# Sends that wait for a later product: pacing GpSimd's scatters in a fused attention and mixture-of-experts block

## The chip, the cores and the metric

The kernel runs on one core of a Trainium2 chip. The metric is the device time of one execution in microseconds, the median of three timed runs. The profile is of another execution, taken by the hardware profiler.

## The reference

Input x is 2 x 1024 tokens of 256 numbers, float32. A small vector gives six modulation rows (shift, scale and gate for each half).

```python
h = _layernorm(x) * (1 + ca) + sa
x = x + ga * attn(h)            # layernorm, causal attention with one head of 256, o_proj, residual
h = _layernorm(x) * (1 + cb) + sb
x = x + gb * ffn(h)

# ffn, on T = 2048 tokens, E = 16 experts, 4 of them for each token, H = 128
probs = softmax(xt @ w_router); top_w, top_i = top_k(probs, 4); top_w /= sum(top_w)
g = silu(xt @ we1[e]) * (xt @ we3[e]) * cw[:, e]
moe_out = sum over e of g @ we2[e]
shared = silu(xt @ ws1) * (xt @ ws3) @ ws2       # width 512
out = shared / 5 + moe_out * 4 / 5
```

## The kernel before, in words

The five engines run programs written out by hand, which meet only at semaphores. Each engine works strictly in the order of its program.

Attention runs over 16 tiles of 128 tokens. Behind each tile the router picks four experts for every token. After each group of four tiles a rank product on TensorE (`rank`, which counts `s_rank_mm` up) gives every token its place among the rows of its expert, and VectorE turns it into four row numbers (`slot_u`, semaphore `s_slots`).

GpSimd then *sends* the tokens: `send` (line 776) issues one indirect DMA for tile t and choice k. It writes 128 rows of `hrow` to the places in the DRAM table `xg_rows` that `slot_u` names. There are 16 x 4 = 64 of them, numbered n = 4t + k. The table `SENDS` puts the first 32 between steps of attention; sends 32 to 63 are issued one behind the other after it. Sends 32 to 47 are the third group (tiles 8 to 11), 48 to 63 the fourth.

Meanwhile TensorE computes the shared part in 16 units n, a block of 512 tokens and a quarter of the width each: `gate_up(n)` (12 matmuls with 512 columns, counts `s_ab`), SiLU on ScalarE, product on VectorE, `down(n)` (8 matmuls, counts `s_y`). Units 2 to 11 stand between attention and the next stage, and in this order: gate_up(3), gate_up(4), the rank product of the last group, down(2), gate_up(5), down(3), gate_up(6), and so on.

Then the routed part. The rows in `xg_rows` are sorted by expert and cut into 79 tiles of 128, two tiles a *pair*, 40 pairs. SyncE loads a pair's rows (line 645). In round n TensorE does the gate/up product of pair n (`rows_gate_up`, 12 matmuls, counts `s_rgu`), the transposes of pair n + 2's rows (`rows_back`, line 2191), the transposes of pair n - 1's product (`g_back`, line 2217) and the down product of pair n - 2 (`rows_down`). A float32 product is split in three (lines 1816 to 1818), the parts high x high, high x low and low x high. For a pair, ScalarE applies SiLU (line 1083) and copies the result y to a buffer in SBUF (line 1092, counts `s_ry`). There are four such buffers, used in a ring, and four more for the last pairs. VectorE computes `r_g` (line 1771).

GpSimd waits for `s_ry` and scatters the pair's y, one indirect DMA a tile (line 817), to the DRAM table `y_rows`, one row for each token and choice. When they have landed, `s_back` goes up and the buffer is free. SyncE loads `y_rows` back in 16 pieces, choice by choice, as soon as enough of the pairs have landed (line 672), and VectorE adds them (line 1497), three of these adds inside the last rounds of pairs; for the last block of 512 tokens TensorE adds two of the choices (line 2004) into the last shared units. VectorE scales and adds to x, and SyncE writes the result.

Of the kernel before, what the change touches and what calls it, by code (L numbers as in the profile page):

```python
# [82 lines left out]
NPAIR = NTL // 2  # L83
# [9 lines left out]
def tiles_of(n):  # L93

    return range(1 if n == NPAIR - 1 else 2)


def loads_of(n):


    return sum(len(tiles_of(m)) for m in range(n % RING, n + 1, RING))


def products(n):


    return sum(1 + len(tiles_of(m)) for m in range(n + 1))

OWN = 6
# [22 lines left out]
NG = TILES // BT  # L134
# [59 lines left out]
SENDS = {9: 4, 10: 4, 11: 4, 12: 4, 13: 4, 14: 4, 15: 4, 16: 4}  # L194
# [41 lines left out]
def adaln_block(nc, x, qkv, o_proj, gamma, beta, w_router, we1, we3, we2, ws1, ws3, ws2, c_in, wmod, out):  # L236
# [3 lines left out]
    with ctx:  # L240
        def sem(name):
            return ctx.enter_context(nc.semaphore(name))
# [253 lines left out]
        def done(eng, stage_, t):  # L496

            if t >= 0:
                eng.wait_ge(tl[stage_], t + 1)
# [4 lines left out]
        s_chosen, s_carry, s_rank_mm, s_slots, s_tv, s_places_mm, s_places = (sem(n) for n in (  # L504
            "chosen", "carry", "rank_mm", "slots", "tile_values", "places_mm", "places"))
# [5 lines left out]
        s_ab, s_y, s_silu, s_g, s_gated, s_shared = (sem(n) for n in (  # L511
            "gate_up_mm", "down_mm", "silu", "g", "shared_gated", "shared_added"))
# [5 lines left out]
        s_rxT, s_rxhi, s_rxlo, s_rgu, s_rsilu, s_rg, s_rgT, s_rghi, s_rglo, s_rdown, s_ry = (sem("r_" + n) for n in (  # L518
            "xT", "xhi", "xlo", "gate_up", "silu", "g", "gT", "ghi", "glo", "down", "y"))
# [29 lines left out]
        def y_of(n):  # L549

            if n < NPAIR - RING:
                return y_sb[:, n % RING]
            return y_own[:, n - (NPAIR - RING)]
# [134 lines left out]
        def _(pool):  # L688
# [73 lines left out]
                                        ).then_inc(tl["resid"], 1)  # L762

            sent = [0]

            def send(count):


                for n in range(sent[0], sent[0] + count):
                    t, k = divmod(n, TOPK)  # L770
                    if n == 0:
                        pool.wait_ge(s_regions, 16 * 5)
                    if k == 0:
                        done(pool, "h2row", t)
                        pool.wait_ge(s_slots, t // BT + 1)
                    nc.gpsimd.indirect_dma_start(  # L776
                        out=xg, out_offset=bass.IndirectOffsetOnAxis(ap=slot_u[:, t, k:k + 1].bitcast(U32), axis=0),
                        in_=hrow[:, t, :], in_offset=None).then_inc(s_sent, 16)
                sent[0] += count

            for s in range(FIRST, LAST + 2):
                if -3 < s < 0:
                    residual(s + 3)
                for m, group in enumerate(norms_of(s)):
                    if s == -3 and m == 1:
                        residual(0)
                    inverse_std(group)
                    for n, t in reversed(group):
                        if n > 1:
                            mean_shift(n, t)  # L790
                if 0 <= s and s + 3 < RESIDUAL_BY_VECTOR:

                    done(pool, "rinv", s - 1)
                    residual(s + 3)
                if s == 3:
                    router_constants()
                if s == 5:
                    token_numbers()
                send(SENDS.get(s, 0))
# [5 lines left out]
            for r in range(RING):  # L805
                nc.gpsimd.memset(sent_all[:, :, r:r + 1], 16.0 * loads_of(NPAIR - RING + r)).then_inc(s_mark_const, 1)
            send(TILES * TOPK - sent[0])


            for n in range(NPAIR):  # L810
                r = n % RING

                pool.wait_ge(s_ry, n + 1)
                if n >= NPAIR - RING:
                    pool.wait_ge(s_back[r], 16 * loads_of(n - RING))
                for i in tiles_of(n):
                    nc.gpsimd.indirect_dma_start(  # L817
                        out=yb, out_offset=bass.IndirectOffsetOnAxis(ap=dest[:, 2 * n + i:2 * n + i + 1].bitcast(U32), axis=0),
                        in_=y_of(n)[:, i, :], in_offset=None).then_inc(s_back[r], 16)
# [1474 lines left out]
```

## Time and profile before

| | |
|---|---|
| timed runs, median of 3 | 339.18 us (338.8 to 339.65) |
| profiled execution, first to last instruction | 380.7 us |
| profiled execution, any other time of it | none on the page |
| TensorE busy | 333.3 us, 88% |
| VectorE busy | 255.2 us, 67% |
| ScalarE busy | 190.3 us, 50% |
| GpSimd busy | 200.8 us, 53% |
| sends of tokens (line 776) | 64, 1.02 us each |
| sends of y (line 817) | 79, 0.98 us each |

The profiled execution is 41.5 us longer than the median of the timed runs. Busy time counts an instruction from start to end, and ends of matmuls are modelled. A wait is put down to the engine that by the profile came last; "remote" is a wait whose releaser the profile does not show.

### The profile page before, as it was taken

What the parts mean: (1) busy time and instruction counts of PE and PEld (TensorE: products, weight loads), DVE (VectorE), ACT (ScalarE), POOL (GpSimd) and SP (SyncE); (2) the same over time, 40 slices, a digit from 0 to 9 for tenths busy, and PEclk for the clock granted to TensorE, in tenths of its full rate; (3) what the DMA queues carried; (4) which work ended last, traced back from release to release, by engine and by line L of the source; (5) the groups of instructions that cost most, each with busy time, mean ns of one, the idle gap of its engine ahead of it and who ended that gap; (6) DMA issues with size and microseconds to landing.
All of it is one profiled execution on the core that took longest, in us unless ns stands there. A gap on an engine that the chain in (4) does not pass through costs nothing.

```text
span 380.7 us, 7758 instructions
## 1 busy us (share of the span) xinstructions
PE 333.3 (88%) x2252; PEld 297.6 (78%) x2252; DVE 255.2 (67%) x806; ACT 190.3 (50%) x440; POOL 200.8 (53%) x285
## 2 busy tenths in 40 slices
PE   8989999999999999868889897788778877887995
PEld 5778898888899898736778796777667767877784
DVE  1889998999887756219986744543454345448797
ACT  2667777767865665414234444443444355346300
POOL 2687754357867655746740064555455545545820
PEclk9999999999999999969999999999999999999999
DMA  8236600002213996322232466556445544788824
GB/s 271 75 104 205 209 17 27 16 31 87 85 65 118 316 312 214 119 85 78 104 117 76 121 209 183 155 171 194 149 124 171 164 133 136 264 302 327 261 86 165
DMA packets 42280, 57.55 MB, mean 151 GB/s; under 512 B 5144, under 2 KB 34592, under 8 KB 42240
## 3 DMA queue, kind: packets, MB, share of 16 engines
q1 hardware_dynamic: 34288, 35.42, 30.7%
q0 software_dynamic: 6864, 19.80, 13.5%
q10 hardware_dynamic: 1088, 1.84, 1.5%
q8 instruction: 20, 0.33, 0.4%
q14 instruction: 20, 0.16, 0.2%
HBM read 32.64 MB, written 24.40 MB: 150 GB/s over the span
## 4 chain that ended last, share of the span: by engine, by line
PE 43%; DVE 27%; issue 13%; another core or an unknown queue 7%; ACT 7%; DMA 1%; POOL 1%; DVEq 0%; ACTq 0%
PE ps L1816 10%; PE ps L1818 10%; PE ps L1817 9%; PE ps L1990 4%; DVE y_in L1497 3%; DVE r_g L1771 2%; DVE gT_lo L1759 2%; ACT r_silu L1083 2%; DVE negmax L1626 2%; PE ps L2191 2%; PE ps L2092 1%; PE ps L1823 1%; DMA wmod_sb<-in_L_wmod_dram 1%; DVE bn L1197 1%
## 5 line engine op out<-in xcount | busy, mean ns | idle before, releaser
L817 POOL DMA_INDIRECT y_rows<-y_sb,aside x72 | 70.5, 980 | 87.9 <-ACT y_sb L1092 71.7
L776 POOL DMA_INDIRECT xg_rows<-hrow,slot_u x64 | 65.6, 1024 | 27.8 <-issue 20.0
L1816 PE MATMUL ps<-rpool 128*128 128x256 f32 (+3 forms) x152 | 49.8, 328 | 2.7 <-DVE rpool L1221 1.1
L1768 DVE TENSOR_TENSOR aside<-ends,aside 128x2 int32<-128x2 int32 (+1 forms) x40 | 6.3, 157 | 62.9 <-ACT r_silu L1083 55.4
L1816 PE MATMUL ps<-w_hi_routed,xT_hi 128*128 x158 | 45.2, 286 | 1.8 <-DVE xT_lo L1752 1.8
L1083 ACT ACTIVATE r_silu<-ps 128x256 f32<-128x256 f32 x40 | 15.8, 395 | 61.4 <-PE ps L1818 51.4
L1818 PE MATMUL ps<-rpool 128*128 128x256 f32 (+3 forms) x152 | 46.0, 302 | 0.0
L1817 PE MATMUL ps<-rpool 128*128 128x256 f32 (+3 forms) x152 | 45.9, 302 | 0.0
L1818 PE MATMUL ps<-w_hi_routed,xT_lo 128*128 x158 | 44.7, 283 | 0.0
L1817 PE MATMUL ps<-w_lo_routed,xT_hi 128*128 x158 | 44.6, 283 | 0.0
L1816 PE MATMUL ps<-w_hi_routed,gT_hi 128*128 x79 | 25.8, 326 | 15.1 <-DVE gT_lo L1759 15.0
L1816 PEld LDWEIGHTS ps<-rpool 128*128 128x128 f32 x152 | 28.8, 190 | 6.0 <-DVE rpool L1221 2.5
L1816 PEld LDWEIGHTS ps<-w_hi_routed,xT_hi 128*128 128x128 f32 x158 | 30.2, 191 | 2.5 <-issue 2.3
L1752 DVE TENSOR_TENSOR xT_lo<-ps,xT_hi 128x512 fp32r<-128x512 f32 x40 | 27.4, 684 | 6.2 <-ACT xT_hi L1071 6.0
L1817 PEld LDWEIGHTS ps<-w_lo_routed,xT_hi 128*128 128x128 f32 x158 | 30.2, 191 | 0.0
L1818 PEld LDWEIGHTS ps<-w_hi_routed,xT_lo 128*128 128x128 f32 x158 | 30.2, 191 | 0.0
L1816 PEld LDWEIGHTS ps<-w_hi_routed,gT_hi 128*128 128x128 f32 x79 | 14.9, 188 | 19.5 <-issue 19.4
L1818 PEld LDWEIGHTS ps<-rpool 128*128 128x128 f32 x152 | 28.8, 189 | 1.1
L1817 PEld LDWEIGHTS ps<-rpool 128*128 128x128 f32 x152 | 28.9, 190 | 0.9
L1816 PE MATMUL ps<-h2T_hi,w_hi_shared 128*128 128x512 f32 x64 | 27.3, 426 | 1.4 <-issue 0.9
L1071 ACT ACTIVATE xT_hi<-ps 128x512 fp32r<-128x512 f32 x40 | 24.4, 612 | 8.0 <-remote 5.8
L1817 PE MATMUL ps<-h2T_lo,w_hi_shared 128*128 128x512 f32 x64 | 25.6, 400 | 2.6 <-issue 2.6
(236 smaller groups left out, 928.8 us busy)
## 6 DMA issues: line engine op xcount, KB each, us to landing
xs<-xg_rows SPq DMA_DIRECT2D x68, 144.0 KB
y_in<-y_rows SPq DMA_DIRECT2D x16, 512.0 KB
xg_rows<-empty SPq DMA_DIRECT2D x4, 576.0 KB, 3.8
x_in<-in_L_attn_x_dram SPq DMA_DIRECT2D x16, 128.0 KB, 2.1
w_raw_routed<-in_L_ffn_we_dram SPq DMA_DIRECT2D x8, 256.0 KB
out_dram<-x SPq DMA_DIRECT2D x14, 128.0 KB, 1.8
xs_own<-xg_rows SPq DMA_DIRECT2D x11, 144.0 KB
wmod_sb<-in_L_wmod_dram ACTq DMA_DIRECT2D x3, 512.0 KB, 6.6
```

Source lines behind the costliest of these rows:

```text
L776: nc.gpsimd.indirect_dma_start(out=xg, out_offset=bass.IndirectOffsetOnAxis(ap=slot_u[:, t, k:k + 1].bitcast(U32), axis=0), in_=hrow[:, t, ...
L817: nc.gpsimd.indirect_dma_start(out=yb, out_offset=bass.IndirectOffsetOnAxis(ap=dest[:, 2 * n + i:2 * n + i + 1].bitcast(U32), axis=0), in_ ...
L1071: nc.scalar.activation(xT_hi[:, n % 2].rearrange("p i c t -> p (i c t)"), ps[:, 6 + n % 2, :], ACT.Copy).then_inc(s_rxhi, 1)
L1083: nc.scalar.activation(r_silu[:, n % 2], ps[:, n % 2, :].rearrange("p (i w) -> p i w", i=2)[:, :, 0:H], ACT.Silu).then_inc(s_rsilu, 1)
L1497: then(nc.vector.tensor_tensor(y[0], y[0], y[k], ALU.add))
L1626: nc.vector.tensor_reduce(negmax[:, t % 4:t % 4 + 1], score_banks(t), AX.X, ALU.max, negate=True).then_inc(tl["negmax"], 1)
L1752: nc.vector.tensor_tensor(xT_lo[:, n % 2].rearrange("p i c t -> p (i c t)"), ps[:, 6 + n % 2, :], xT_hi[:, n % 2].rearrange("p i c t -> p ...
L1759: nc.vector.tensor_tensor(gT_lo[:, n % 2].rearrange("p i t -> p (i t)"), ps[:, 2 + n % 2, 0:2 * P], gT_hi[:, n % 2].rearrange("p i t -> p ...
L1816: nc.tensor.matmul(dst, w[0], x_[0], start=first, stop=False)
L1817: nc.tensor.matmul(dst, w[0], x_[1], start=False, stop=False)
L1818: return nc.tensor.matmul(dst, w[1], x_[0], start=False, stop=last)
L1990: last = nc.tensor.matmul(to, unit(n)[1][:, tok], w_raw_s[:, e, W2:WX], start=(e == 0 and b < NB - 1 and j % 2 == 0), stop=(e == SH - 1), ...
```

## The change

Two places, both in GpSimd's program. Before the indirect DMA of sends 36, 38, 40, 42, 44 and 46 a wait is put for a product of TensorE: gate_up(2), gate_up(3), the last rank product, down(2), gate_up(5) and down(3), in this order. And the sends of pair n wait, beside `s_ry`, for the gate/up product of pair n + 3 (`s_rgu` at n + 4, for the last pairs at 40).

```diff
+PACE = 4
...
+            LATE = sum(SENDS.values())
+
+            def after_product(n):
+
+                if n == LATE + 4:
+                    pool.wait_ge(s_ab, 3)
+                if n == LATE + 6:
+                    pool.wait_ge(s_ab, 4)
+                if n == LATE + 8:
+                    pool.wait_ge(s_rank_mm, NG)
+                if n == LATE + 10:
+                    pool.wait_ge(s_y, 3)
+                if n == LATE + 12:
+                    pool.wait_ge(s_ab, 6)
+                if n == LATE + 14:
+                    pool.wait_ge(s_y, 4)
...
                         pool.wait_ge(s_slots, t // BT + 1)
+                    after_product(n)
                     nc.gpsimd.indirect_dma_start(
...
                 pool.wait_ge(s_ry, n + 1)
+                pool.wait_ge(s_rgu, min(n + PACE, NPAIR))
```

`LATE` is 32, the number of sends that the table places. No engine's order of instructions changes. What changes are the waits on GpSimd. Its program in the third and the start of the fourth group of sends, before:

```order
L802 IOTA first_of 128x40 [waits t_scores]
L806 MEMSET sent_all 128x1 x4
L776 DMA xg_rows<-hrow,slot_u 32896x288 [waits slots,t_h2row]
L776 DMA xg_rows<-hrow,slot_u 32896x288 x3
L776 DMA xg_rows<-hrow,slot_u 32896x288 [waits slots,t_h2row]
L776 DMA xg_rows<-hrow,slot_u 32896x288 x3
```

And after (`gate_up_mm`, `down_mm` and `rank_mm` are `s_ab`, `s_y` and `s_rank_mm`):

```order
L822 IOTA first_of 128x40 [waits t_scores]
L826 MEMSET sent_all 128x1 x4
L796 DMA xg_rows<-hrow,slot_u 32896x288 [waits slots,t_h2row]
L796 DMA xg_rows<-hrow,slot_u 32896x288 x3
L796 DMA xg_rows<-hrow,slot_u 32896x288 [waits gate_up_mm,slots,t_h2row]
L796 DMA xg_rows<-hrow,slot_u 32896x288
L796 DMA xg_rows<-hrow,slot_u 32896x288 [waits gate_up_mm]
L796 DMA xg_rows<-hrow,slot_u 32896x288
L796 DMA xg_rows<-hrow,slot_u 32896x288 [waits rank_mm,slots,t_h2row]
L796 DMA xg_rows<-hrow,slot_u 32896x288
L796 DMA xg_rows<-hrow,slot_u 32896x288 [waits down_mm]
```

Every second send of the third group from the fifth on is now held for a product. The sends of the first two pairs' y on GpSimd, before:

```order
L776 DMA xg_rows<-hrow,slot_u 32896x288 [waits slots,t_h2row]
L776 DMA xg_rows<-hrow,slot_u 32896x288 x3
L817 DMA y_rows<-y_sb,aside 11264x256 [waits r_y]
L817 DMA y_rows<-y_sb,aside 11264x256
L817 DMA y_rows<-y_sb,aside 11264x256 [waits r_y]
```

And after (`r_gate_up` is `s_rgu`):

```order
L796 DMA xg_rows<-hrow,slot_u 32896x288 [waits slots,t_h2row]
L796 DMA xg_rows<-hrow,slot_u 32896x288 x3
L838 DMA y_rows<-y_sb,aside 11264x256 [waits r_gate_up,r_y]
L838 DMA y_rows<-y_sb,aside 11264x256
L838 DMA y_rows<-y_sb,aside 11264x256 [waits r_gate_up,r_y]
```

The first of a pair's two sends carries the second wait; the other follows it as before.

## Rows read from the trace of the kernel before

**Rows 1.** The page, span of the profiled execution.

```profile
span 380.7 us, 7758 instructions
```

**Rows 2.** Busy time: length, PE, PEld, DVE, ACT, POOL, clock, DMA, GB/s.

```profile
0.00:158.00 158.00, 149.70 (x1032) 135.07 (x1032) 124.07 (x419) 103.49 (x251) 97.37 (x183) 1.00 0.40 134
158.00:172.00 14.00, 9.27 (x30) 6.15 (x30) 2.50 (x12) 3.65 (x6) 7.25 (x8) 0.76 0.24 91
172.00:225.00 53.00, 47.85 (x274) 41.24 (x273) 43.85 (x112) 21.96 (x39) 21.13 (x20) 1.00 0.34 109
225.00:347.00 122.00, 98.26 (x780) 91.40 (x780) 56.98 (x225) 52.92 (x128) 62.59 (x66) 1.00 0.59 189
```

**Rows 3.** Groups by line in 225:347 us: busy, mean ns | idle before, releasers.

```profile
L1092 ACT ACTIVATE y_sb<-ps 128x512 f32<-128x512 f32 x32 | 19.4, 606 | 9.3 <-PE ps L1818 8.0 <-issue 1.2
L1083 ACT ACTIVATE r_silu<-ps 128x256 f32<-128x256 f32 x32 | 12.7, 398 | 52.9 <-PE ps L1818 43.0 <-remote 9.9
```

**Rows 4.** Timeline of TensorE in the loop: start, length, instruction.

```profile
217.43 0.38 PE L2217 MATMUL ps<-ident,r_g 128*128 128x128 f32 x2
...
225.30 0.28 PE L1818 MATMUL ps<-w_hi_routed,xT_lo 128*128 x1
...
225.85 0.38 PE L2217 MATMUL ps<-ident,r_g 128*128 128x128 f32 x2
```

**Rows 5.** Timeline of ScalarE, the same stretch.

```profile
228.92 0.38 ACT L1083 ACTIVATE r_silu<-ps 128x256 f32<-128x256 f32 x1 [4.15 <-PE ps L1818]
```

**Rows 6.** Timeline of GpSimd, the same stretch.

```profile
223.15 0.96 POOL L817 DMA_INDIRECT y_rows<-y_sb,aside  x1 [1.49 <-ACT y_sb L1092]
...
226.94 0.96 POOL L817 DMA_INDIRECT y_rows<-y_sb,aside  x1 [0.30 <-issue]
```

**Rows 7.** Timelines of TensorE and VectorE around 156 to 170 us.

```profile
156.60 0.40 PE L1818 MATMUL ps<-h2T_hi,w_lo_shared 128*128 128x512 f32 x1
...
158.09 0.41 PE L1941 MATMUL ps<-carry,ones 128*128 128x64 f32 x2
...
170.05 0.22 DVE L1315 TENSOR_TENSOR above<-ps,region 128x64 f32<-128x64 f32 x1 [11.37 <-remote]
```

**Rows 8.** Timeline of GpSimd: sends 36, 47 and 48.

```profile
152.49 0.96 POOL L776 DMA_INDIRECT xg_rows<-hrow,slot_u  x1 [0.30 <-issue]
...
166.43 0.96 POOL L776 DMA_INDIRECT xg_rows<-hrow,slot_u  x1 [0.30 <-issue]
173.05 0.96 POOL L776 DMA_INDIRECT xg_rows<-hrow,slot_u  x1 [5.66 <-DVE slot_u L1347]
```

**Rows 9.** Timeline of TensorE: shared units, late and freely issued.

```profile
158.34 1.73 PE L1990 MATMUL ps<-w_raw_shared,act_g 128*128 128x256 f32 x7
...
173.34 0.47 PE L1816 MATMUL ps<-h2T_hi,w_hi_shared 128*128 128x512 f32 x1 [0.44 <-DVE act_g L1461]
...
190.07 0.58 PE L1816 MATMUL ps<-h2T_hi,w_hi_shared 128*128 128x512 f32 x1
...
194.53 0.58 PE L1816 MATMUL ps<-h2T_hi,w_hi_shared 128*128 128x512 f32 x1
```

**Rows 10.** Timelines: a send of y, loads of y, and a reader.

```profile
347.88 0.96 POOL L817 DMA_INDIRECT y_rows<-y_sb,aside  x1 [0.30 <-issue]
...
351.26 0.80 SPq L672 DMA_DIRECT2D y_in<-y_rows  x2
...
356.99 0.32 SPq L672 DMA_DIRECT2D y_in<-y_rows  x1
...
371.03 1.89 PE L2004 MATMUL ps<-y_in,ident 128*128 128x256 f32 x8
```

**Rows 11.** The first loads of rows, their reader, and a landing time.

```profile
196.94 17.33 SPq L645 DMA_DIRECT2D xs<-xg_rows  x12
...
207.50 0.60 PE L2191 MATMUL ps<-ident,xs 128*128 128x128 f32 x4
...
xg_rows<-empty SPq DMA_DIRECT2D x4, 576.0 KB, 3.8
```

## The prediction, as it was put on record

> **What bounds the kernel now.** I read the span first, against the timed runs, because they disagree: the profiled execution took 380.7 us [rows 1] and the page gives no other time for it, while the three timed runs have a median of 339.18 us. The two differ by 41.5 us, twelve per cent of a timed run, so before any term is costed it must be known where the profiled execution spends those 41.5 us. Then I took the busy time by stage. In rows 2 TensorE is busy 149.7 of the first 158 us (attention and its neighbours) and 47.9 of 53 us in 172:225, but only 9.3 of 14 us in 158:172 and 98.3 of 122 us in 225:347, the loop over pairs. These two stretches are the odd ones.
>
> The loop first. Rows 3 give who waits in it: ScalarE waits 43.0 + 9.9 us before its first operation of a pair (the SiLU of line 1083) for TensorE's gate/up product. TensorE's own records say that this product was not late. In rows 4 the last matmul of one product starts at 225.30, TensorE goes on at once with the transposes, and yet the SiLU that needs it starts at 228.92 [rows 5], after 4.15 us of idle time. So ScalarE sees TensorE's signal about 3.5 us after the matmul that carries it. Rows 6 show what is going on meanwhile: GpSimd issues four sends back to back from 223.15, the last ends at 227.90, and the SiLU starts 1.0 us later. From there it repeats every second pair. What it costs comes from the spacing of pairs: the transposes of line 2217 are at 217.43 and 225.85 three pairs apart [rows 4], 2.81 us a pair, with TensorE issuing without a gap. Later, 32 pairs fill 122 us (line 1092 has one instruction a pair) [rows 2, 3], 3.81 us a pair. The excess is 122 - 32 x 2.81 = 32.1 us.
>
> The other stretch shows the same thing once and longer. The rank product's last matmuls start at 158.09 [rows 7]; VectorE, which waits for nothing else, reads the result at 170.05, after 11.4 us of waiting [rows 7], eleven of them past the product. GpSimd's sends ran back to back, 1.27 us apart, from 152.49 or before to 167.39 [rows 8]. From 158.34 to 173.34 TensorE does a down, a gate/up and a down of shared units; freely issued a gate/up and a down take 4.5 us (190.07 to 194.53), and a down alone 1.5 us (the row at 158.34 has seven of its eight matmuls in 1.73 us, the last one's latency in it) [rows 9], 6.0 us in all, so 15.0 - 6.0 = 9.0 us are lost. Both together: 32.1 + 9.0 = 41.1 us, and 380.7 - 41.1 = 339.6 us, 0.4 us from the median of the timed runs. So I read the timed executions as those in which TensorE's signals are not late: pairs every 2.81 us, TensorE issuing almost without a gap, and VectorE's chain of adds at the end. No trace can show this, since each is of a profiled execution; it rests on the sum.
>
> The Trainium skill (NOTIFIC — the notification-queue block, 7.1) says that the unit which writes trace records holds its producers back rather than lose a record inside. That would be a way for lateness to exist in profiled executions alone; no row here shows that unit. Its page on the runtime (Runtime: NRT & Kernel Launch, on the profile's total time) puts a constant of about 6.2 us between a profile's total and the reported time; by that alone the timed run would be 374.5 us, and 339.18 contradicts it.
>
> **The change, part by part.** No engine's order of instructions changes; 46 waits are added, one for each of 40 pairs and six in the third group, all on GpSimd. What stands behind a waiting send on GpSimd is only more sends, so each term is a delay of sends and of whoever needs what was sent.
>
> Pairs' sends: the send of pair n now also waits for product n + 3. TensorE's order after down(n) is gate/up(n + 3) at once. That is 12 matmuls at 0.12 us, 1.44 us. The copy of y costs ScalarE 0.61 us [rows 3], and a send follows it by 0.3 us at best, the gap between sends [rows 6]. So in a timed execution the wait holds each send by about 1.44 - 0.9 = 0.5 us, call it 0.6 with the semaphore: the same for every pair, hence once and not 40 times. GpSimd needs 1.27 + 1.27 = 2.53 us for a pair's two sends [rows 6] in a period of 2.81 us, and has 0.28 us to spare, so it keeps up.
>
> Who waits for a send? First ScalarE, which may overwrite a buffer four pairs later. Released at t, the second send starts at t + 1.4. For its landing take rows 10: pair 34's last send starts at 347.88 and the loads of rows of y that wait for it start at 351.26, 3.4 us. It has landed by t + 4.8. Copy n + 4 comes three products after t, then transposes and down: 3 x 2.81 + 1.4 = t + 9.8. The slack is 5.0 us, cost nothing. By the Trainium skill (DMA: Bandwidth & Descriptors, Anatomy of one DMA) a transfer of 128 KB on this path takes about 2.0 + 0.3 = 2.3 us, which would make the slack 6.1 us; an upper end of 3.4 is what the trace has. Second, the loads of y back to SBUF: the last one starts at 356.99, and its reader, the product of line 2004 on TensorE, at 371.03 [rows 10]. That is 14 us, and by rows 11 a load of 576 KB lands in 3.8 us, these of 512 KB in about as much. Cost nothing up to some 10 us of delay. For the last pairs the wait is min(n + 4, 40), and there TensorE has passed the product before y is ready.
>
> The third group's sends: in rows 8, send 36 was issued at 152.49 and then one each 1.27 us, so 38 at 155.02, 40 at 157.55, 42 at 160.09, 44 at 162.62, 46 at 165.16. Without lateness the products are done by 153.9 (38: one gate/up, 3.0 us, before the end of the next, whose last matmul starts at 156.60), 36's before that, 158.5 (40, the rank) [rows 7], and then, by the pace of rows 9, 159.9 (42), 162.8 (44), 164.3 (46). Only 40 waits, 1.0 us, and the rest move with it: the sends end 1.0 us later. Their reader is the first load of rows, issued at 196.94, and the transposes at 207.50 that need it [rows 11]. A load of 576 KB lands in 3.8 us on this queue [rows 11], so this one of 144 KB in less. The slack is 207.5 - 196.9 - 3.8 = 6.8 us here. In a timed execution TensorE is 9.0 us earlier and GpSimd's fourth group 5.4 us (the ranks no longer come at 170, and the queue goes on at 167.7 instead of 173.05 [rows 8]): 3.2 us before the change, 2.2 us after. Cost nothing, and if the slack were misjudged by 3 us, 1 us. Even with the rank signal as late as in the profile, send 44 would wait to 170.3 and the fourth group start 2.5 us later, still within the 6.8 us.
>
> The sum: 0 (buffers) + 0 (loads of y) + 0 to 1.0 us (the third group), of which I take 0, the nearest rows giving slack throughout. Against the profiled execution's own time the change is likewise worth nothing unless it removes lateness, which is a rival for timed runs and an expectation for the profile, below. The forecast is the median, **339.2 us**, with its own range of 338.2 to 340.2 us.
>
> **Rivals.** (A) *The late signals exist in timed executions too, in part, and breaking up GpSimd's bursts removes them: faster.* For it: lateness ends each time about a microsecond after a burst ends [rows 5, 6], and the new waits do cut bursts of four sends into two and two, at a point where a signal from TensorE has just got through. Against it: with all lateness taken off, my sum is still 0.4 us above the median, so some can only be left in timed runs if other stretches are shorter there. TensorE's idle time outside the two stretches and the tail is 8.3 us before 158 and 5.2 us in 172:225 [rows 2]; if all of it were gone in timed runs, 13.5 - 0.4 = 13.1 us of lateness could remain. A quarter of that, 3.3 us, gives **335.9 us**.
>
> (B) *GpSimd becomes the bound of the loop: slower.* It has 0.28 us to spare per pair. Place: the sends of pairs in the loop. If a send behind a wait on two engines costs more than that extra, because it can't be issued while the one before is written, the sends fall behind by the difference each pair, 36 times, until ScalarE waits for a buffer. At 0.35 us extra this is 0.07 x 36 = 2.5 us: **341.7 us**. It decides only from 0.28 us per pair. Against it: the gap between sends is 0.30 us in a burst [rows 6] whether the second has a wait of its own (a new pair's) or not.
>
> (C) *The waits are always met, the change does nothing at all.* Same time as the forecast, 339.2 us; the 0.6 us above says that they do hold, but only just.
>
> **How the numbers follow.** What this kernel's measurement can tell from no change is about 0.3%, 1.0 us. The forecast gets 0.48 and C 0.10, together 0.58 for no difference. A gets 0.26, B 0.16. So faster 0.26, same 0.58, slower 0.16. For eight in ten the range reaches most of A and B: 335.8 to 341.0 us, short of B's price by little since B has the smallest chance.
>
> **What would show it.** In the profile after, sends of pairs should come in twos, each pair starting after a product's end. If bursts cause the lateness, the SiLU's waits (52.9 us in rows 3) nearly vanish, pairs come every 2.8 us and the span falls to about 341 to 346 us while the timed median stays: I give that 0.6. If pairs still come every 3.8 us and the span stays near 380, bursts are not the cause. ScalarE's copy of y waiting for a send, or the load of y behind line 2004 arriving after TensorE is ready, would prove the zero costs wrong. The forecast is wrong if the timed median moves by more than 1 us; a gain would say that my split of the 41.5 us is wrong and lateness is a part of ordinary runs.

## The result, and the profile after

The change made the kernel slower. Four timed executions of the changed kernel have a median of 343.45 us (343.06 to 343.86), four of the kernel before one of 339.41 us. The medians are 4.0 us apart, and the ratio, 1.0108 [1.0088, 1.0129] with its 95% interval, gives 3.7 us. Timed a second time, beside the experiments, they had 343.15 against 340.07 us, 1.0082 [1.0051, 1.0113]. The forecast was 339.2 us in a range up to 341.0, so it was wrong, and on the side that it thought least likely.

The profiled execution of the changed kernel shows nothing unusual. The page, its span, and two of its costliest groups:

```profile
span 341.8 us, 7794 instructions
...
L838 POOL DMA_INDIRECT y_rows<-y_sb,aside x72 | 69.7, 968 | 50.5 <-issue 28.7
L796 POOL DMA_INDIRECT xg_rows<-hrow,slot_u x64 | 67.8, 1060 | 24.2 <-issue 19.7
...
L1104 ACT ACTIVATE r_silu<-ps 128x256 f32<-128x256 f32 x40 | 15.3, 383 | 37.1 <-PE ps L1839 37.0
```

The span is 341.8 us where [rows 1] had 380.7, and all 40 SiLUs together wait 37.1 us, where the 32 in [rows 3] waited 52.9. Is that the change's doing? It is not, as a new profile of the kernel before shows. These are the busy times by stage of that profile (length; busy time and instructions of TensorE, its weight loads, VectorE, ScalarE, GpSimd; clock, DMA share, GB/s):

```profile
158.00:172.00 14.00, 14.00 (x68) 11.98 (x68) 11.28 (x34) 6.20 (x9) 10.93 (x11) 1.00 0.29 112
172.00:207.00 35.00, 32.34 (x175) 27.14 (x174) 29.32 (x68) 12.22 (x21) 15.66 (x14) 1.00 0.36 117
207.00:309.00 102.00, 101.92 (x862) 100.87 (x861) 64.84 (x253) 66.52 (x144) 67.97 (x70) 1.00 0.73 232
```

And the same of the changed kernel:

```profile
158.00:172.00 14.00, 14.00 (x68) 11.84 (x67) 11.46 (x36) 6.20 (x9) 9.94 (x9) 1.00 0.25 96
172.00:207.00 35.00, 30.10 (x157) 25.23 (x156) 27.39 (x59) 11.09 (x18) 18.05 (x16) 1.00 0.35 117
207.00:309.00 102.00, 101.54 (x861) 100.56 (x859) 64.32 (x253) 66.11 (x144) 65.25 (x68) 1.00 0.72 226
```

In both, TensorE is busy throughout 158:172, where [rows 2] had 9.27 of 14 us, and nearly throughout 207:309, in the loop. The difference that is the change's own stands in 172:207: 32.34 us busy before, 30.10 after. That is 2.2 us, and it lies at one place. First GpSimd in the changed kernel, at sends 39 to 43 (start, length, instruction, idle time before it and what ended it):

```profile
156.58 0.96 POOL L796 DMA_INDIRECT xg_rows<-hrow,slot_u  x1 [0.30 <-issue]
159.63 0.96 POOL L796 DMA_INDIRECT xg_rows<-hrow,slot_u  x1 [2.09 <-PE ps L1962]
160.89 0.96 POOL L796 DMA_INDIRECT xg_rows<-hrow,slot_u  x1 [0.30 <-issue]
162.16 1.56 POOL L796 DMA_INDIRECT xg_rows<-hrow,slot_u  x1 [0.30 <-issue]
164.02 1.43 POOL L796 DMA_INDIRECT xg_rows<-hrow,slot_u  x1 [0.30 <-issue]
```

Send 40 waits for the rank product, 2.09 us instead of the usual 0.30. No other of the six waits holds anything: all later sends follow at 0.30 us. Then the last of the 64 sends and what hangs on it, from the chain of waits of the same kernel (start, length, what):

```profile
193.02 3.08 DMA xg_rows<-hrow,slot_u
...
196.85 2.16 DMA xs<-xg_rows
199.01 0.04 issue
199.06 0.67 PE ps L2212 x4
```

GpSimd's sends, the landing of the last, the load of the first rows and their transposes are on the critical chain. TensorE's side of it, the last shared unit and the transposes that answer to line 2191 in [rows 11]:

```profile
192.21 4.49 PE L2011 MATMUL ps<-w_raw_shared,act_g 128*128 128x256 f32 x20
...
199.06 0.66 PE L2212 MATMUL ps<-ident,xs 128*128 128x128 f32 x4 [2.37 <-DMA xs<-xg_rows]
```

And in the new profile of the kernel before:

```profile
192.39 4.49 PE L1990 MATMUL ps<-w_raw_shared,act_g 128*128 128x256 f32 x20
...
197.10 0.66 PE L2191 MATMUL ps<-ident,xs 128*128 128x128 f32 x4 [0.23 <-DMA xs<-xg_rows]
```

The wait for the first rows grew from 0.23 to 2.37 us. Note that it was not zero before: in this profile the kernel before has no slack between the first load and TensorE, and its critical chain runs through the same sends, load and transposes. The experiments below put to the test that this is the whole matter.

### The profile page after: what moved, and what is told of

Same layout as the page of the kernel before. It is cut to its first block, busy times and chain, and to the rows that moved or that the text cites. A ratio compares the mean times of both kernels' runs of the same rounds, so it can differ in the third digit from the quotient of the medians.

```text
span 341.8 us, 7794 instructions
## 1 busy us (share of the span) xinstructions
PE 324.5 (95%) x2252; PEld 297.5 (87%) x2252; DVE 255.8 (75%) x806; ACT 195.9 (57%) x440; POOL 202.2 (59%) x285
## 3 DMA queue, kind: packets, MB, share of 16 engines
q10 hardware_dynamic: 1088, 1.84, 1.7%
## 4 chain that ended last, share of the span: by engine, by line
PE 52%; DVE 19%; issue 11%; POOL 10%; ACT 4%; DMA 3%; DVEq 0%; SPq 0%; ACTq 0%; POOLq 0%
PE ps L1837 13%; PE ps L1838 12%; PE ps L1839 12%; POOL xg_rows L796 7%; PE ps L2212 5%; DVE y_in L1518 3%; PE ps L2238 2%; DVE negmax L1647 2%; PE ps L1844 1%; PE ps L2113 1%; DMA wmod_sb<-in_L_wmod_dram 1%; PE ps L1946 1%; DVE bn L1218 1%; DVE y_in L1528 1%; PE ps L2011 1%
## 5 line engine op out<-in xcount | busy, mean ns | idle before, releaser
L838 POOL DMA_INDIRECT y_rows<-y_sb,aside x72 | 69.7, 968 | 50.5 <-issue 28.7
L796 POOL DMA_INDIRECT xg_rows<-hrow,slot_u x64 | 67.8, 1060 | 24.2 <-issue 19.7
L1104 ACT ACTIVATE r_silu<-ps 128x256 f32<-128x256 f32 x40 | 15.3, 383 | 37.1 <-PE ps L1839 37.0
L1839 PE MATMUL ps<-h2T_hi,w_lo_shared 128*128 128x512 f32 x64 | 25.1, 392 | 0.0
```

Source lines behind the costliest of these rows:

```text
L796: nc.gpsimd.indirect_dma_start(out=xg, out_offset=bass.IndirectOffsetOnAxis(ap=slot_u[:, t, k:k + 1].bitcast(U32), axis=0), in_=hrow[:, t, ...
L838: nc.gpsimd.indirect_dma_start(out=yb, out_offset=bass.IndirectOffsetOnAxis(ap=dest[:, 2 * n + i:2 * n + i + 1].bitcast(U32), axis=0), in_ ...
L1104: nc.scalar.activation(r_silu[:, n % 2], ps[:, n % 2, :].rearrange("p (i w) -> p i w", i=2)[:, :, 0:H], ACT.Silu).then_inc(s_rsilu, 1)
L1839: return nc.tensor.matmul(dst, w[1], x_[0], start=False, stop=last)
```

## The experiments

Executions of one kernel differ by some 2 us from the start on: the first four matmuls, fed by a weight from DRAM (line 1823 in e5, 1822 in e11), start at 4.97 and take 3.75 us in e5's profile, and start at 5.39 and take 1.96 us in e11's. So I compare profiles by distances, measured from the start of the group of 20 matmuls above, called *the mark* here. Each timed median stands beside that of the kernel before, timed together with it, ratios with their 95% intervals.

| label | edit | timed, before | ratio | sends end | first load | transposes |
|---|---|---|---|---|---|---|
| e5_before_again | none | 340.36, 340.07 | 1.0003 [0.9984, 1.0022] | -0.8 | +1.7 | +4.7 |
| e6_after_again | the whole change | 343.15, 340.07 | 1.0082 [1.0051, 1.0113] | +2.4 | +4.1 | +6.9 |
| e1_pairs_only | pairs' wait | 340.20, 339.84 | 1.0013 [0.9993, 1.0033] | -0.8 | +1.5 | +4.3 |
| e2_group_only | the six waits | 342.37, 339.84 | 1.0078 [1.0049, 1.0108] | +2.5 | +4.1 | +6.9 |
| e3_pairs_pace3 | pairs' wait, product n + 2 | 340.00, 339.84 | 1.0005 [0.9991, 1.0019] | -0.8 | +1.6 | +4.4 |
| e4_no_rank | the change less the rank wait | 341.02, 339.84 | 1.0033 [1.0015, 1.0051] | +0.5 | +2.2 | +4.8 |
| e7_rank_only | rank wait at send 40 | 342.89, 340.07 | 1.0082 [1.0052, 1.0112] | +2.4 | +4.1 | +7.0 |
| e8_down_at_40 | a later wait at send 40 | 344.97, 340.07 | 1.0160 [1.0135, 1.0184] | +3.7 | +5.4 | +8.1 |
| e9_rank_at_42 | rank wait at send 42 | 340.00, 340.05 | 1.0005 [0.9986, 1.0024] | -0.8 | +1.6 | +4.6 |
| e10_pairs_pace5 | pairs' wait, product n + 4 | 341.50, 340.05 | 1.0069 [1.0042, 1.0095] | -0.7 | +1.3 | +4.3 |
| e11_no_read_splits | no two-input subtractions | 339.28, 340.05 | 0.9989 [0.9969, 1.0009] | -2.3 | +1.3 | +4.3 |
| e12_no_read_splits_rank | the same, rank wait at send 40 | 340.07, 340.05 | 1.0014 [0.9993, 1.0036] | -1.1 | +1.4 | +4.3 |

The last three columns are microseconds from the mark: the end of send 63, the issue of the first load of rows, and the first transposes. From the second column to the third pass 1.7 us wherever the sends end behind the mark, but 2.1 to 2.5 us where they end 0.7 to 1.1 us ahead of it, and 3.6 us in e11. So the load that opens the routed part did not come before +1.3 in any of these profiles, and the sends had some 0.4 to 0.8 us to spare ahead of it; between the load and TensorE there was nothing to spare. The section on the slack comes back to this.

### Which of the two parts costs

The first four runs take the change apart. e1_pairs_only keeps the wait of the pairs' sends and leaves the six waits uncalled:

```diff
                     if k == 0:
                         pool.wait_ge(s_slots, t // BT + 1)
-                    after_product(n)
                     nc.gpsimd.indirect_dma_start(
```

> The pairs' wait alone (product n + 3), no waits in the third group. Theory T (third group): the 4.0 us of the change come from GpSimd's queue of 32 sends, whose end starts the routed part; then this kernel is within 1 us of the kernel before, 339.4 us, and its profile shows no late signals in the loop (pairs every 2.8 us), but still the hole near 158 to 172 us. Rival P (pairs): the held sends cost something in the loop or the tail; then 341 to 343.5 us.

Measured: 340.20 against 339.84 us, no difference that can be told. The profile has its first transposes at +4.3 without any wait. The hole near 158 to 172 us that was expected of it isn't there: TensorE is busy 13.99 of these 14 us.

e2_group_only does the reverse:

```diff
                 pool.wait_ge(s_ry, n + 1)
-                pool.wait_ge(s_rgu, min(n + PACE, NPAIR))
```

> The six waits of the third group alone. T: 342.5 to 343.5 us, all or nearly all of the cost. P: at most 1.8 us over the kernel before, 341.2 us, since GpSimd lost only 1.8 us at the rank wait in the profile after. In the profile the stretch 158 to 172 us is full and the loop shows pairs every 3.8 us again.

Measured: 342.37 against 339.84 us, 2.5 us slower. The loss is in the group of six waits. Its profile shows pairs every 2.8 us, where 3.8 were expected, although the pairs' sends wait for y alone as before. So nothing of the odd profile of before came back.

e3_pairs_pace3 is e1 with one product less to wait for:

```diff
-PACE = 4
+PACE = 3
```

> The pairs' wait with product n + 2 (always done before the down product of pair n), none in the third group: a wait that holds nothing. If a wait for two semaphores costs GpSimd anything by itself, this kernel shares e1's cost; T and P both say 339.4 us. If its profile has late signals in the loop as the kernel before, it is the delay of the send and not the wait that keeps them away.

Measured: 340.00 us, 0.2 us from e1, which is not a difference here.

e4_no_rank has the whole change, without one of its six waits:

```diff
-                if n == LATE + 8:
-                    pool.wait_ge(s_rank_mm, NG)
```

> The changed kernel without the wait for the rank product before send 40. T: the rank wait is the only one that held a send (2.09 us idle before send 40 at 159.63), so its removal gives back 1.5 to 2.1 us: 341.5 us; the next wait, down(2) before send 42, may take a part of it over. P: the same, with the rest of the 4.0 us in the pairs.

Measured: 341.02 us, 2 us below e6, so most of the loss hangs on the rank wait. What remains is 1.2 us over before, with the transposes only 0.1 us later than in e5; e1's 0.4 us for the pairs' wait is a part of it, the rest is not split. Send 42 now waits 0.5 us (0.81 instead of 0.30) for the down product, as a row of its trace shows:

```profile
160.38 0.96 POOL L794 DMA_INDIRECT xg_rows<-hrow,slot_u  x1 [0.81 <-PE ps L2009]
```

### Is the odd profile a matter of the kernel

e5_before_again and e6_after_again are the two kernels unchanged, profiled once more.

> The kernel before once more, unchanged, for a trace of it. Theory U (the profiled execution of 380.7 us was an unusual one): span near 338 us, no late signals, pairs every 2.8 us, GpSimd's bursts as long as ever. Rival L (bursts make TensorE's signals late whenever a trace is taken): span near 380 us again. Time 339.8 us by both. In the trace by theory T, TensorE does not wait, or under 0.3 us, for the first load of rows.

Measured: 340.36 us timed, span 339.6 us in the profile. This is what the prediction could not show. The kernel before, with its bursts of sends, runs in a profile just as in timed executions: the execution behind this span was itself timed at 341.33 us. The lateness belonged to one execution. Thirteen other profiled executions of these kernels have spans from 336.6 to 343.1 us. Neither the profiler nor the bursts bring it about by themselves; what did is open.

> The changed kernel once more, to set it beside e1 and e2 on one chip: 342.4 to 343.6 us. If the two parts add up, third group 2.6 us and pairs 0.3 to 0.9 us give 342.7 to 343.3 us.

Measured: 343.15 us, transposes at +6.9 after a wait of 2.4 us: the result repeats.

### Is it the one wait, and by how much

e7_rank_only has one wait and nothing else of the change:

```diff
+                if n == LATE + 8:
+                    pool.wait_ge(s_rank_mm, NG)
```

> Only the wait for the rank product before send 40. Theory T: the same 1.8 us of GpSimd's queue is lost as with all six waits, so 341.7 to 342.7 us, equal to the six waits' 342.4. If another of the six costs too, less: 341 us.

Measured: 342.89 against 340.07 us, 1.0082, the same ratio as the whole change had beside it, and 0.2 us over the range expected. One wait of 46 makes the loss. The row that counts in its trace:

```profile
198.98 0.66 PE L2201 MATMUL ps<-ident,xs 128*128 128x128 f32 x4 [2.54 <-DMA xs<-xg_rows]
```

e8_down_at_40 holds the same send longer, up to the down product behind the rank:

```diff
-                    pool.wait_ge(s_rank_mm, NG)
+                    pool.wait_ge(s_y, 3)
```

> The dose: the one wait before send 40 is put for down(2), which is done about 1.7 us after the rank product, so GpSimd's queue is held about 3.0 us instead of 1.8. Theory T (no slack is left between the queue of sends and the first load): 1.0 to 1.4 us more than the rank wait alone, 343 to 343.9 us. If the cost of a wait is something other than the delay of the queue, it is the same as the rank wait's.

Measured: 344.97 us, 4.9 us over before, more than I expected of it. Its send 40 is held 3.6 us, 1.8 more than with the rank:

```profile
161.14 0.96 POOL L786 DMA_INDIRECT xg_rows<-hrow,slot_u  x1 [3.87 <-DVE slot_u L1357]
```

(The wait is put down to VectorE's `slot_u`, which came last by the profile. The same wait for `slot_u` stands before this send in the kernel before, where it holds nothing; only the product is new.) The transposes come 3.4 us later than in e5, as one would expect of 3.6 us. The rest is a second price. TensorE has now been idle 3.62 us, and its clock falls:

```profile
200.04 1.12 PE L2201 MATMUL ps<-ident,xs 128*128 128x128 f32 x4 [3.62 <-DMA xs<-xg_rows]
202.66 0.97 PE L2201 MATMUL ps<-ident,xs 128*128 128x128 f32 x4
204.90 0.60 PE L2201 MATMUL ps<-ident,xs 128*128 128x128 f32 x4
```

Busy time around it, where the last figures of a line are clock, DMA share and GB/s:

```profile
196.00:200.00 4.00, 0.42 (x2) 0.02 (x1) 0.24 (x1) 0.00 (x0) 0.00 (x0) 1.00 0.46 139
200.00:204.00 4.00, 3.96 (x17) 3.49 (x18) 2.11 (x5) 0.60 (x1) 0.00 (x0) 0.58 0.70 207
204.00:208.00 4.00, 2.42 (x20) 2.19 (x20) 3.57 (x11) 1.36 (x3) 0.00 (x0) 1.00 0.21 62
```

The granted clock is 0.58 in 200:204, which is mostly the lower of the two levels, 1.2 GHz. By the first transposes of g (line 2227), 17.1 us behind the mark against 12.6 in e5, the lag has grown from 3.4 to 4.5 us. In the changed kernel, after 2.37 us of idle time, the clock granted in 199:203 is 1.00.

e9_rank_at_42 has the same wait two sends later, when the product is done:

```diff
+                if n == LATE + 10:
+                    pool.wait_ge(s_rank_mm, NG)
```

> The rank wait alone, put two sends later, before send 42, which is due 1.3 us after the rank product. Theory T (only the delay of the queue costs): nothing is held, 339.6 to 340.6 us, the kernel before. If the wait itself costs, 342.9 us as with the wait before send 40.

Measured: 340.00 against 340.05 us, and all sends from 40 on follow at 0.30 us. A wait that is met costs nothing that can be told here; it is the held time that costs.

### Where the slack had gone

The account of the sends' lengths, from GpSimd's timeline in e5, at sends 43 to 45 and 52 to 56. The prediction had put every send at 1.27 us:

```profile
161.81 0.96 POOL L776 DMA_INDIRECT xg_rows<-hrow,slot_u  x1 [0.30 <-issue]
163.08 1.69 POOL L776 DMA_INDIRECT xg_rows<-hrow,slot_u  x1 [0.30 <-issue]
165.07 0.96 POOL L776 DMA_INDIRECT xg_rows<-hrow,slot_u  x1 [0.30 <-issue]
...
174.08 1.50 POOL L776 DMA_INDIRECT xg_rows<-hrow,slot_u  x1 [0.30 <-issue]
175.88 0.96 POOL L776 DMA_INDIRECT xg_rows<-hrow,slot_u  x1 [0.30 <-issue]
177.15 1.43 POOL L776 DMA_INDIRECT xg_rows<-hrow,slot_u  x1 [0.30 <-issue]
178.88 0.96 POOL L776 DMA_INDIRECT xg_rows<-hrow,slot_u  x1 [0.30 <-issue]
180.15 1.63 POOL L776 DMA_INDIRECT xg_rows<-hrow,slot_u  x1 [0.30 <-issue]
```

Most sends take 0.96 us, but seven take 1.11 to 1.69, 3.6 us more in sum. VectorE at the same times:

```profile
162.12 2.69 DVE L1453 TENSOR_TENSOR w_lo_routed<-w_raw_routed,w_hi_routed 128x768 fp32r<-128x768 f32 x3
...
172.93 1.81 DVE L1453 TENSOR_TENSOR w_lo_routed<-w_raw_routed,w_hi_routed 128x768 fp32r<-128x768 f32 x2
...
176.79 1.83 DVE L1453 TENSOR_TENSOR w_lo_routed<-w_raw_routed,w_hi_routed 128x768 fp32r<-128x768 f32 x2
...
179.13 2.69 DVE L1453 TENSOR_TENSOR w_lo_routed<-w_raw_routed,w_hi_routed 128x768 fp32r<-128x768 f32 x3
```

The long sends lie beside these subtractions, which read two tensors from SBUF. What decides is which of the two starts first. Send 43 is under way when the subtractions of 162.12 start, and keeps its 0.96 us; send 44 starts among them and takes 1.69. e11_no_read_splits takes them away by putting zeros in their place, so it leaves the low parts of the routed weights out of the result:

```diff
-                nc.vector.tensor_tensor(w_lo_r[:, e, :], w_raw_r[:, e, :], w_hi_r[:, e, :].bitcast(F32),
-                                        ALU.subtract).then_inc(s_wlo_r, 1)
+                nc.vector.memset(w_lo_r[:, e, :].bitcast(F32), 0.0).then_inc(s_wlo_r, 1)
```

> The kernel before, with VectorE filling the low parts of the routed weights with zeros instead of computing them (this leaves the low parts out of the result). Theory S: sends take 1.4 to 1.7 us instead of 0.96 when VectorE's subtraction of two tensors in SBUF runs beside them; without it all sends take 0.96 us, the last one ends about 3.5 us earlier, and TensorE waits for no load. The time falls by at most 1 us, since TensorE had almost no wait to lose. Rival: the long sends come from something else (ScalarE's copies, DMA traffic) and stay.

Measured: 339.28 us, 0.9989 of before, not to be told from it; there the wait of 0.23 us for the first rows was all there was to gain. The sends end 2.3 us ahead of the mark, 1.6 us earlier than in e5 and not the 3.5 that were expected: of sends 40 to 63 two are still long (1.84 and 1.77 us) and one takes 1.02. The two start while another instruction with two inputs in SBUF runs. GpSimd's row and VectorE's:

```profile
186.13 1.77 POOL L776 DMA_INDIRECT xg_rows<-hrow,slot_u  x1 [0.30 <-issue]
```

```profile
185.84 1.22 DVE L1478 TENSOR_TENSOR x<-x,gated 128x1024 f32<-128x1024 f32 x1
```

The Trainium skill (GPSIMD Engine Reference, 8. Key points) says that GpSimd shares its SBUF interfaces with VectorE and that they contend when a VectorE instruction has two SBUF inputs. The trace agrees: up to 1.84 us beside such instructions, 0.96 us beside a memset. It also agrees that both inputs must lie in SBUF. Send 62 of e11 starts in the middle of VectorE's products with one input in PSUM (`ps`), and is not longer:

```profile
184.87 0.96 POOL L776 DMA_INDIRECT xg_rows<-hrow,slot_u  x1 [0.30 <-issue]
```

```profile
184.52 1.28 DVE L1472 TENSOR_TENSOR gated<-ps,gate_b 128x512 f32<-128x512 f32 x2
```

The length of a long send follows from its start. The instruction of 185.84 ends at 187.06, and the send that started in it ends 0.84 us later, at 187.90. Of sends 40 to 63 in the 13 undisturbed profiles, 92 start more than 0.05 us into a subtraction of line 1453 or the residual add of line 1479 (e5's numbers): each ends at least 0.83 us behind it. Another 69 start first and run into such an instruction, and take 0.96 to 0.97 us.

That e11's load is issued only 0.4 us earlier than e5's, though its sends end 1.6 us earlier, has another cause. The DMA queues of e11, in 188.4:190.9 and in 189.1:190.9 (queue, kind: packets, MB, share of the 16 DMA engines):

```profile
q8 instruction: 1, 0.02, 3.8%
```

```profile
q0 software_dynamic: 3, 0.01, 2.8%
```

One packet of the kind "instruction" takes 3.8% of 16 engines for 2.5 us, which is 1.5 us of one of them, and the last three packets of the sends pass behind 189.1, more than 1 us after GpSimd's last send has ended. Each of these profiles has such a packet near the mark. That it holds up the last rows, and so the load, is an inference; no run moves it.

e12_no_read_splits_rank adds the wait of e7 to e11. It is the test of the whole theory: if the wait costs only because the slack is gone, it must be cheap where there is slack.

> The same, with the rank wait before send 40 (the costly one of the change). Theories T and S together: the 3.5 us that shorter sends give back cover the 1.8 us of the wait, TensorE does not wait for the first load, and the time is that of the same kernel without the wait, within 0.5 us. If S is wrong, 2.5 us more than it.

Measured: 340.07 us, 1.0014 of before, where the same wait cost 1.0082 in e7. Send 40 is held as before:

```profile
159.28 0.96 POOL L786 DMA_INDIRECT xg_rows<-hrow,slot_u  x1 [2.07 <-PE ps L1950]
```

and the transposes are at +4.3, as in e11, behind no wait. The median is 0.8 us above e11's, where 0.5 was expected at most, but within what the intervals leave open; from the mark to the end the two profiles are 146.4 and 146.3 us. So the held time itself is harmless. It costs where the end of the sends is what TensorE waits for.

### How much more the pairs' sends can be held

e10_pairs_pace5 is e1 with a product more:

```diff
-PACE = 4
+PACE = 5
```

> Pairs' sends wait for product n + 4 (one more), no waits in the third group: each send is held 2.8 us longer. By the slack of 5.0 us at the ring of buffers it costs no more than the wait for n + 3, 340.2 to 340.8 us, and the loop from the first to the last transpose of line 2217 takes 107.4 to 107.8 us as with n + 3 (106.8 without). If the slack at the ring or at the loads of y is smaller than I took it, 342 us and more.

Measured: 341.50 against 340.05 us, 1.0069 [1.0042, 1.0095], so this expectation missed. The prediction had 5.0 us of slack behind the wait for product n + 3, and one product more takes 2.8. The chain of waits names what is late, the landing of a scatter that frees a buffer:

```profile
293.59 7.26 DMA y_rows<-y_sb,aside
...
300.93 0.60 ACT y_sb L1112
...
304.81 3.85 DMA y_rows<-y_sb,aside
308.66 6.39 DMA y_in<-y_rows
```

The group of ScalarE's copies of y in 206:325 says how often: they wait 3.7 us in all for such a landing, a releaser that the same view names in none of the other kernels.

```profile
L1112 ACT ACTIVATE y_sb<-ps 128x512 f32<-128x512 f32 x36 | 21.6, 599 | 6.9 <-DMA y_rows<-y_sb,aside 3.7 <-PE ps L1838 1.5
```

A scatter that starts at 293.59 lands 7.3 us later, not the 3.4 us taken from [rows 10]. From first transposes to the last transposes of g the loop is 116.0 us long, against 115.1 in e5 and 114.8 in e3.

No version beats the kernel before. e11 is not slower, but it leaves work out.

## Why the prediction failed, step by step

**The sum of the lateness held, its split only roughly.** Lateness of 32.1 + 9.0 us was taken off the profiled time and 339.6 us left; the new profile of the kernel before has a span of 339.6 us and pairs every 2.8 us. The timed executions are those without lateness, as forecast, and rival A, which wanted some of it in timed runs, is false. The agreement to the tenth is luck. The mark stands at 203.17 us in the first profile and at 192.39 in e5, so 10.8 us were lost ahead of it and not 9.0, and 30.3 behind it and not 32.1; the two errors cancel in the sum. The slack below takes only the 9.0. The expectation that the new profile would have a span of 341 to 346 us came true with 341.8, but its reason fell: e5 and e2 have bursts and no lateness.

**The pairs' sends held.** The prediction put them at 0 us, and e1 gives +0.4 us [-0.2, +1.1], not told from nothing. The profiles with this wait have loops of 115.3 to 115.7 us from the first transposes to the last of g, those without 114.4 to 115.1 and once, behind the clock's fall in e8, 115.7. So a price of up to some 0.7 us may be there; the timed runs leave it open. The size of the slack was too large: 5.0 us by a landing of 3.4, where a scatter late in the loop took 7.3. The loads of y were taken at about 3.8 us and take 6.2 on e5's page (median), which left the zero there right.

**GpSimd did not become the bound (B).** It waits 50.5 us before the sends of y in the changed kernel, and the gaps stay at 0.58 us for most pairs. The kernel became slower by another mechanism than the rival on that side.

**The step that failed** is the one that reads: "The slack is 207.5 - 196.9 - 3.8 = 6.8 us here. In a timed execution TensorE is 9.0 us earlier and GpSimd's fourth group 5.4 us (...): 3.2 us before the change, 2.2 us after. Cost nothing". Measured, the slack before was -0.2 us: TensorE waits 0.23 us in e5. The prediction did price the case that its slack was off by 3 us, at 1 us, and then put the term at 0. The slack was off by 3.4 us. Each part of the sum, against e5:

- TensorE's due time. The sum has 207.5 - 9.0 = 198.5; with the shared units through at 192.39 + 4.49 it is 196.9, 1.6 us earlier. The odd profile had lost more ahead of the mark than was charged.
- The first load. The sum has 196.9 - 5.4 = 191.5; it was issued at 194.11, 2.6 us later. Of this 1.2 us is send 48, which starts at 168.87 instead of 167.7: 0.5 because the whole group starts later, 0.7 because send 44 takes 1.69 us. The other 1.4 us arise between send 48 and the load: 0.5 in long sends, which take 2.8 us over 0.96 each in this group where the odd profile had 2.3, and 0.8 between the end of the last send and the load, 2.5 us instead of 1.7.
- The landing. 3.8 us was taken, 3.0 passed from load to transposes, 0.8 us in favour.

Together 3.2 - 1.6 - 2.6 + 0.8 = -0.2 us, which is what e5 shows. The error was to carry a distance over from a disturbed execution by subtracting a round figure on either side, when the answer is a difference of two such figures.

**The held time was also too small.** The prediction had 1.0 us: product done at 158.5, send due at 157.55. The product's last matmul ends at 158.40 + 0.41 = 158.81 in the changed kernel, and the send starts 0.82 us later, at 159.63, where 157.84 was due: 1.8 us. The signal's way to GpSimd was left out. (It is not the same everywhere: 0.82 us at send 40, which waits for three things, `rank_mm`, `slots` and `t_h2row`, but 0.27 us at send 42 of e4, at 160.38, which waits for the product alone, done there at 160.11.) On top of it the shifted sends start within VectorE's two-input instructions more often: nine of 24 are long, 5.0 us more than at 0.96 each, against 3.6 in e5. So the last send ends 1.8 + 1.4 = 3.2 us later from the mark (-0.8 to +2.4), the first load is issued 2.4 us later, since 0.8 of the 3.2 had been spare ahead of it, and the transposes come 2.1 us later. With no slack to swallow it, that is the loss, and timed it is 2.5 to 2.8 us in e2 and e7. From the mark to the end pass 146.4 us in e9, 146.6 in e3, 147.2 in e5 and 147.3 in e1, but 149.2 in e7, and 149.6 and 150.1 in the two profiles of the whole change. So e7's loss is 2.0 to 2.8 us by the profiles, too. The excess of the first timing, 3.7 us, is about 1 us over that; it lies within the intervals and what the pairs' wait may add, and is not shown apart.

## What to carry to other kernels

A wait put into a queue that runs back to back shifts all that stands behind it, so its price is read at the last reader of that queue and not at the waiting instruction. Find that reader, and see whether it already waits, even for 0.2 us, in a profile whose span agrees with the timed runs. If the span and the timed time disagree by more than a few microseconds, take another profile before a slack is worked out from it. Here the sum of the corrections was right, its two parts were 1.8 us off, and a slack of 3.2 us that rested on one of them was not there.

## What the runs showed of the hardware

- An indirect DMA of GpSimd takes 0.96 us to issue. If it starts more than 0.05 us into a VectorE instruction with two large inputs in SBUF (128x768 or 128x1024), it ends at least 0.83 us behind that instruction, 1.04 to 1.84 us in all; if it starts first, it keeps its 0.96 us.
- From the end of the last send to the first load that waits for all of them were 1.7 us, and 2.1 to 3.6 us where the last rows passed beside a packet of 0.02 MB of the kind "instruction" (the link is inferred).
- After 3.62 us without work TensorE's granted clock was 0.58 over the next 4 us, and four transposes took 1.12 instead of 0.66 us; after 2.37 us it stayed at 1.00.
- A scatter of 128 rows of y landed 3.4 us after its issue in one place and 7.3 us in another.
- From a matmul's end to the send that waits for it were 0.82 us where the send has three waits, 0.27 us where it has one.
- One execution of 14 profiled ones saw TensorE's signals up to 11 us late, and took 41 us more. Its cause is open.
